# Key-major cross attention: scores straight behind the values product, both projections at the quarter's end

## The reference

```python
q = _split_heads(jnp.einsum('bnd,df->bnf', x, Wq))          # 16 heads of 64
kv = jnp.einsum('bmc,cf->bmf', context, Wkv)
k, v = jnp.split(kv, 2, axis=-1)
...
k = jnp.concatenate((nk, k), axis=-2)                        # one null key
v = jnp.concatenate((nv, v), axis=-2)
sim = jnp.einsum('bhid,bhjd->bhij', q * scale, k)
attn = jax.nn.softmax(sim, axis=-1)
out = jnp.einsum('bhij,bhjd->bhid', attn, v)
out = jnp.einsum('bnf,fd->bnd', out, Wout)                   # then layer norm
```

## Time and profile before

| | |
|---|---|
| median of 3 runs | 5403.31 us (5402.94 to 5409.03) |
| the profiled execution's time | 5403.9 us |
| its span | 5402.1 us |
| last cross attention, first to last peak transpose | 3175.7 to 4984.5 us |
| TensorE busy, whole span | 4622.2 us (86%) |
| VectorE busy | 3458.3 us (64%) |
| ScalarE busy | 2525.0 us (47%) |
| GpSimd busy | 1360.3 us (25%) |
| mean granted TensorE clock | 0.895 of full speed |

### The profile page before, as it was taken

How to read it: one execution, slowest core, us unless ns; L and a number is a source line. 1 busy time by engine, 2 the same in 40 slices (tenths; PEclk the granted TensorE clock), 3 DMA queues, 4 the chain that set the end, 5 groups by cost and what they waited for, 6 DMA issues and landing times. The chain is left out here.

```text
span 5402.1 us, 94417 instructions
## 1 busy us (share of the span) xinstructions
PE 4622.2 (86%) x30135; PEld 2795.7 (52%) x30135; DVE 3458.3 (64%) x7765; ACT 2525.0 (47%) x4776; POOL 1360.3 (25%) x1426
## 2 busy tenths in 40 slices
PE   3699999977959998658888789999999999999554
PEld 2244444436824444326666456666666666666342
DVE  3577777763256665563333357887878787788546
ACT  3466666642436666313333245555555555555220
POOL 0100000000000000001111036666656656666000
PEclk7899999988979999757777889999999999999657
DMA  4211111100022221000000010000000000000001
GB/s 155 56 46 46 46 52 46 40 17 18 18 72 78 79 78 34 5 18 0 0 0 0 7 49 13 1 13 1 13 13 1 13 1 13 1 1 1 5 4 39
DMA packets 134437, 148.22 MB, mean 27 GB/s; under 512 B 25048, under 2 KB 106552, under 8 KB 133848
## 3 DMA queue, kind: packets, MB, share of 16 engines
q1 hardware_dynamic: 134088, 145.01, 8.9%
q10 hardware_dynamic: 144, 0.52, 0.0%
HBM read 129.85 MB, written 15.66 MB: 27 GB/s over the span
## 5 line engine op out<-in xcount | busy, mean ns | idle before, releaser
L753 DVE TENSOR_REDUCE att_peak.1<-psS 128x1 f32<-128x512 f32 (+1 forms) x1024 | 620.7, 638 | 176.1 <-PE psS L635 146.4
L735 ACT ACTIVATE att_probT.1<-psT 128x512 f32<-128x512 f32 (+1 forms) x1024 | 555.2, 567 | 317.7 <-PE psT L659 312.1
L738 ACT ACTIVATE att_probT.2<-psT,att_key_bias.1 128x256 f32<-128x256 f32 (+1 forms) x832 | 344.8, 471 | 159.4 <-PE psT L661 159.3
L2595 POOL TENSOR_TENSOR key_sums_0.1<-key_sums_0.1,prob_0.1 128x512 f32<-128x512 f32 x256 | 402.3, 1572 | 28.7 <-POOL key_sums_0.1 L2595 0.4
L674 PE MATMUL psM<-att_probT.1,head_values.1 128*32 128x256 f32 (+1 forms) x3840 | 403.5, 391 | 0.1
L2595 POOL TENSOR_TENSOR key_sums_1.1<-key_sums_1.1,prob_1.1 128x512 f32<-128x512 f32 x256 | 386.2, 1509 | 28.7 <-POOL key_sums_1.1 L2595 0.4
L635 PE MATMUL psS<-key_stack.1,query_stack.1 96*128 96x512 bf16 (+1 forms) x1024 | 359.4, 372 | 27.0 <-DMA query_stack.1<-query_parts 25.7
L757 DVE CUSTOM_DVE_ANT_0 att_masked.1<-psS,mask_added.1 128x512 f32<-128x512 f32 (+1 forms) x512 | 290.7, 573 | 135.8 <-issue 129.2
L659 PE MATMUL psT<-query_stack.1,key_stack.1 128*128 128x256 bf16 (+1 forms) x1920 | 360.4, 274 | 12.9 <-ACT query_stack.1 L728 1.0
L2434 ACT COPY prob_0.1<-psS 128x1024 f32<-128x1024 f32 (+1 forms) x224 | 203.7, 954 | 323.2 <-PE psS L2333 323.1
L2434 ACT COPY prob_1.1<-psS 128x1024 f32<-128x1024 f32 (+1 forms) x224 | 203.7, 954 | 296.3 <-PE psS L2333 296.3
(11 more groups left out here) (670 smaller groups left out, 9734.7 us busy)
## 6 DMA issues: line engine op xcount, KB each, us to landing
key_stack.1<-key_parts SPq DMA_DIRECT2D x384, 87.0 KB
key_stack.2<-key_parts SPq DMA_DIRECT2D x128, 150.1 KB
ctx_rows.1<-in_ctx_dram SPq DMA_DIRECT2D x8, 1536.0 KB
key_parts<-split_parts.1 SPq DMA_DIRECT2D x8, 1200.8 KB, 5.7
mask_flags.1<-in_mask_BxS_ik_dram SPq DMA_DIRECT2D x8, 800.5 KB, 6.2
key_stack.2<-key_parts SPq DMA_DIRECT2D x64, 100.1 KB
query_stack.1<-query_parts SPq DMA_DIRECT2D x384, 12.0 KB
ctx_keys_0.1<-in_ctx_dram SPq DMA_DIRECT2D x4, 768.0 KB
```

The source lines that it names most:

```text
L735: last = exp(self.probT[0:w, q % 2, blks[0]:blks[-1] + 1, :].rearrange("p b q -> p (b q)"), self.k.psT[0:w, i % 2, 0:len(blks) * S], ACT.Exp)
L738: last = exp(self.probT[0:w, q % 2, blk, :], self.k.psT[0:w, i % 2, n * S:(n + 1) * S], ACT.Exp, bias=self.bias[0:w, q, blk:blk + 1])
L753: nc.vector.tensor_reduce(self.peak[:, s, c:c + 1], scores, AX_X, ALU.max).then_inc(self.peak_done.sem, 1)
L2595: nc.gpsimd.tensor_tensor(acc, acc, own[:, h, c * BANK:(c + 1) * BANK], ALU.add).then_inc(self.summed.sem, 1)
```

## The change

In each quarter the scores now come directly behind the values product (and, in the first quarter, the peak transpose), then the spread of the shift, then value and key projections together. On VectorE the copy of the first value piece moves behind the first head's four lowers. ScalarE's and GpSimd's orders, the other places of VectorE's copies, the banks and the sizes stay as they are.

```diff
@@ pe_run
                 if softmax and g == 0:
                     self.pe_turn_peak(pe, i - 1)
-                for name in self.due(i, 2 * g):
-                    self.pe_project(pe, name)
-                if softmax and g == 0:
-                    self.pe_spread_shift(pe, i - 1)
                 if scores:
                     for s in self.of_run(g):
                         self.pe_score(pe, i, s)
-                for name in self.due(i, 2 * g + 1):
-                    if name is not None:
-                        self.pe_project(pe, name)
+                if softmax and g == 0:
+                    self.pe_spread_shift(pe, i - 1)
+                for at in (2 * g, 2 * g + 1):
+                    for name in self.due(i, at):
+                        if name is not None:
+                            self.pe_project(pe, name)
                 if meets and g == 2:
                     self.pe_total(pe, i - 2)
@@ dve_run
             if softmax:
                 self.dve_shift(dve, i - 1)
-            self.dve_take_at(dve, i, 0)
             if softmax:
                 for part in range(4):
                     self.dve_lower(dve, i - 1, 0, part)
+            self.dve_take_at(dve, i, 0)
             if scores:
                 self.dve_raise(dve, i, 1)
```

## The result

| | before | after |
|---|---|---|
| median of 6 runs each | 5403.12 us (5398.82 to 5409.63) | 5425.09 us (5415.61 to 5429.49) |
| ratio | | 1.0036, 95% interval 1.0023 to 1.0049 |
| span of the profiled execution | 5402.1 us | 5422.8 us |

The account below looks back on a forecast made before the run. TensorE was taken to bound the stage, VectorE close behind. Plain rounds +5.0, 14 context rounds +6.0 and 7 third context rounds -0.5 gave +10.5 on 5403.9 us: 5414 us, range 5388 to 5430.

Parts of the forecast that it names:

- VectorE's tail: VectorE's work from raise 4 to the peak's end, 7.74 us at unchanged durations; claimed to eat TensorE's saving.
- TensorE's saving: Fewer array shape changes: 0.19 us in each of three quarters, 0.58 per plain round, leaving TensorE alone at 27.09 us.
- Rival 1: VectorE's tail stays under TensorE's time and the saving arrives: -25.3 us, 5379; chance 0.20 for whole or half.
- rival (2): Tail at unchanged durations: plain rounds -0.05 us each, +3.8 in all, 5408; chance 0.22, shared with a slightly better phase.
- The walk's 27.82: Plain round followed step by step with VectorE and GpSimd taking turns: next transpose at 27.82 us, +0.15 per round.
- The third value copy stands ahead of raise 4: VectorE copies the third value projection at 19.22 us, so raise 4 starts at 19.83 instead of 19.60.
- with its turns raise 3 ends at 17.78: Plain round, GpSimd first: raise 2 due at 14.03, raise 3 ending at 17.78 us after turns with GpSimd's sums.
- the term of 5.0: Loss in plain rounds: 33 rounds of 0.15 us each, 5.0 us in all.
- context rounds, +0.43 and -0.07: Rounds that also transpose context: +0.43 us in each of 14, -0.07 in each of 7 of the third kind.
- the key projection behind context on `psM`: Quarter two: key projection starts 1.27 us after the context transpose instead of 0.45 after value projection, a 0.82 us stall.
- ScalarE's copy of context ahead of its copy of the scores: Quarter three of context rounds: context's copy at 21.35 us, scores' copy at 21.83, so raise 4 at 22.88.
- Rival 3: Raise 1 goes before GpSimd's first sum: plain rounds 28.22 us, +0.55 each, 23.7 in all, 5428; chance 0.20 including worse phases.

Follow-up runs that it names:

- the pair with small sums: Changed kernel and kernel before, each with GpSimd's sums cut to 8 columns: 5366.5 and 5369.2 us, plain rounds 27.03 and 27.67 us.
- the last two kernels: Changed kernel, raise 1 before first value copy, context copy before raise 3, context transpose before value projection; with ScalarE's scores copies first 5369.14 us, without 5371.5 us.

## Why the prediction came out as it did

The forecast was 5414 us in a range of 5388 to 5430, with a chance of 0.39 for slower and 0.41 for no change beyond 0.2%; measured are 5425 and slower. The mechanism held: TensorE saves what was forecast and VectorE's tail eats it. The size did not. The change costs twice the forecast, 20.8 us of the stage against 10.5, and all of it in context rounds, while the plain rounds, forecast at half of the loss, became 1.0 us faster in all. That 5425 lies in the range is owed to its width, which was there for the phase of GpSimd's sums in plain rounds, and so in part to luck. The sums are right to 0.02 (three times 0.19 was put at 0.58, and 17.13 + 0.45 + 0.82 + 0.45 at 18.83).

- **TensorE's saving, 0.58 in a plain round.** Right: 7.51 for a quarter, 1.88 from values product to scores, and 0.64 where nothing else was late; the first quarter, put at nothing, gave 0.05 of it. Rival 1 (the saving arrives) failed because of VectorE and GpSimd, shown by the pair with small sums.
- **VectorE's tail takes over.** Right in place and time: raise 4 at 19.77 (19.83), the next transpose at 27.61 to 27.65, with one round at 28.15. By unchanged durations I had 27.62, and that rival (2) is what plain rounds did, though not with unchanged durations: raise 4 takes 1.43 instead of 1.38. The walk's 27.82 was off.
- **The cause I gave for the tail was too narrow.** "The third value copy stands ahead of raise 4" is true and worth 0.17 us. Moving it made plain rounds 0.6 us longer. What fills VectorE are the waits in its turns with GpSimd, 5.1 us of a round.
- **The step that failed: "with its turns raise 3 ends at 17.78".** At the seam between the two heads' sums a waiting raise does not get the turn: it waits for the tail and for the next sum. Raise 3 ended at 18.99. I had taken the end of the tail for a free moment, though the seam stood in the trace of before. In plain rounds the 1.2 us vanished in the wait for the value copy, and the later sums met raise 4 a little better than walked (it ends at 21.20, not 21.40), so the term of 5.0 became -1.0.
- **The mis-sized term: context rounds, +0.43 and -0.07; measured +1.01 and +1.10.** The late raise 3 holds up VectorE's copy of context (18.93, where a raise 3 that ends at 17.78 would put it 1.2 us earlier), and this one holds TensorE by bank 0 for 0.6 to 1.45 us. My walk had the value projection wait for nothing. Moving that copy alone took back 19 us. Of the two waits I did price, the key projection behind context on `psM` came as forecast, 1.28 from transpose to projection for 1.27, and is real: the last two kernels show it. The other, ScalarE's copy of context ahead of its copy of the scores, holds raise 4 up as forecast but is not on the path, 0.05 us of a round.
- **Rival 3 (raise 1 wins the tie)** did not happen in the changed kernel; GpSimd won. Where raise 1 does go first, by the swap with the copy, plain rounds are 27.46 and not the 28.22 that this rival has; its price had the wrong sign, as far as that kernel can tell. I had taken the tie as a matter of phase, not as a second VectorE loss that the change brings along.

What stays open: why the phase of the sums turns out better or worse in one kind of round than in another was read off the traces, not forecast; the variation of the rest of the program between 3586 and 3604 us is not explained; and the swaps were not tried on TensorE's old order.

## What to carry to other kernels

A reordering on the busiest engine saves only down to the next engine's loop from round to round; work out that loop's length, with its waits for another engine's turns in it, before counting the saving. When projections are put side by side, look at whose bank they share and at the copies that empty it: a piece that was parted from its bank's next user by other work should be issued first, not next to it. And where two engines take turns, the first instruction of a burst can matter: starting VectorE's instruction half a microsecond ahead of GpSimd's burst took back the whole 21 us that the change had cost.

## What the runs showed of the hardware

- 16 matmul records with a full array between two blocks on a halved one took 1.98 us instead of 1.79, so the two changes of shape cost 0.19 us together, and from weights of 128 rows x 64 columns to 64 x 128 costs the same as to a full array (1.88 us either way for 16 records).
- VectorE's maximum of two SBUF tensors (128x1024) takes 1.22 us alone, about 2.1 when it waits for one of GpSimd's sums and 2.79 when two stand back to back; the waits count as VectorE's busy time. With the sums cut to 8 columns every one of them took 1.22, and VectorE was busy 5.1 us less of 24.6 in a round.
- TensorE idle for 3.70 us in a stage of granted clock 1.00 came back at 0.50 and took 3.78 us for what takes 2.05; idle times of 1.45 us in the changed kernel's stage left the clock at 1.00. With TensorE's order alone, idle times of 2.24 us were followed by 0.50 in four rounds and by 1.00 in three; that is the spread of its second kind of context round, 31.8 to 34.7 us.
